# Loading a head group's q and k by twelve sixteen-row DMAs in place of sixteen

## The reference, cut to what matters

```python
x = x + layernorm(attention(layernorm(x)))      # causal, 16 heads, per batch of 1024 tokens
x = x + layernorm(moe(layernorm(x)))            # 8 experts, top 2, 256 -> 1024 -> 256
# attention, per head h:
attn = softmax(mask(q_lat[h] @ c_kv.T / 4)) ;  y[h] = (attn @ c_kv) @ v_eff[h]
```

## Time and profile before

| what | value |
|---|---|
| median of three runs | 1412.35 us |
| the profiled execution, its own time | 1411.45 us |
| its span in the profile | 1409.8 us |
| PE busy | 1124.4 us (80%) |
| DVE busy | 817.6 us (58%) |
| ACT busy | 654.0 us (46%) |
| POOL busy | 586.1 us (42%) |
| DMA moved | 190.07 MB, 135 GB/s on average |

### The profile page before, as it was taken

One profiled execution on the slowest core, in us unless ns is written; L12 is line 12 of the kernel. 1 busy time (PEld: TensorE's weight loads), 2 busy tenths in 40 slices (PEclk: granted clock), 3 DMA queues, 4 the chain that ended last, 5 costly groups with the idle time before them and its releaser, 6 DMA issues. The chain is left out here.

```text
span 1409.8 us, 26281 instructions
## 1 busy us (share of the span) xinstructions
PE 1124.4 (80%) x7809; PEld 834.2 (59%) x7809; DVE 817.6 (58%) x2044; ACT 654.0 (46%) x1111; POOL 586.1 (42%) x675
## 2 busy tenths in 40 slices
PE   5956299998999899999983443099999999999910
PEld 3523255555555555555541433099999999999910
DVE  5626166665666566666622975055555555555567
ACT  2620055554555455555564543044444444444444
POOL 4204055555555355555574577412222222222227
PEclk9977599999999999999997555589999999999965
DMA  4953133343344434443223514342344142341173
GB/s 153 375 217 122 45 136 128 130 141 132 135 143 144 145 127 144 143 144 126 91 91 122 198 67 134 95 157 84 129 168 168 45 168 91 122 168 46 45 253 119
DMA packets 93853, 190.07 MB, mean 135 GB/s; under 512 B 27604, under 2 KB 58596, under 8 KB 85508
## 3 DMA queue, kind: packets, MB, share of 16 engines
q1 hardware_dynamic: 82912, 163.09, 32.7%
q0 software_dynamic: 7680, 22.09, 4.6%
q10 hardware_dynamic: 3176, 3.84, 0.9%
HBM read 109.44 MB, written 79.02 MB: 134 GB/s over the span
## 5 line engine op out<-in xcount | busy, mean ns | idle before, releaser
L775 ACT ACTIVATE att_pt<-att_ps_s 128x1024 f32<-128x1024 f32 (+3 forms) x384 | 305.4, 813 | 250.8 <-PE att_ps_s L690 248.3
L805 DVE TENSOR_REDUCE att_pm<-att_ps_m 128x1 f32<-128x512 f32 (+1 forms) x512 | 298.5, 649 | 125.4 <-PE att_ps_m L657 115.5
L1513 ACT ACTIVATE moe_hf<-moe_ps_h,moe_b 128x256 f32<-128x256 f32 x288 | 136.9, 475 | 222.9 <-PE moe_ps_h L1469 216.2
L653 PE MATMUL att_ps_m<-att_k,att_q 128*128 128x512 f32 (+3 forms) x576 | 202.6, 409 | 39.4 <-DMA att_v<-vs 31.8
L603 POOL TENSOR_SCALAR_AFFINE_SELECT att_pt<-att_pt 128x512 f32<-128x512 f32 x128 | 80.7, 636 | 293.9 <-ACT att_pt L775 293.9
L690 PE MATMUL att_ps_s<-att_q,att_k 128*128 128x512 f32 (+3 forms) x576 | 169.3, 378 | 12.3 <-ACT att_pt L775 6.3
L653 PEld LDWEIGHTS att_ps_m<-att_k,att_q 128*128 128x128 f32 x576 | 114.5, 202 | 81.1 <-DVE att_pm L805 44.1
L1422 POOL DMA_INDIRECT ys<-moe_o,moe_home x72 | 74.0, 1028 | 186.3 <-DVE moe_o L1552 173.3
L690 PEld LDWEIGHTS att_ps_s<-att_q,att_k 128*128 128x128 f32 x576 | 92.0, 191 | 64.0 <-issue 30.8
L1546 DVE TENSOR_TENSOR moe_hTl<-moe_hf,moe_hTh 128x256 fp32r<-128x256 f32 x288 | 123.9, 430 | 10.0 <-DVE moe_hTh L1544 0.2
L657 PE MATMUL att_ps_m<-keep_future,keep_identb 128*128 128x128 bf16 x512 | 118.4, 238 | 0.0
(11 more groups left out here) (196 smaller groups left out, 2587.4 us busy)
## 6 DMA issues: line engine op xcount, KB each, us to landing
att_raw<-in_w SPq DMA_DIRECT2D x16, 1024.0 KB, 5.4
ws<-att_raw_hi SPq DMA_DIRECT2D x16, 1024.0 KB, 5.0
ws<-att_raw SPq DMA_DIRECT2D x16, 1024.0 KB, 6.8
moe_rows<-xs SPq DMA_DIRECT2D x38, 258.0 KB, 2.7
weights_w_0h<-ws SPq DMA_DIRECT2D x8, 1024.0 KB
weights_w_0l<-ws SPq DMA_DIRECT2D x8, 1024.0 KB
att_q<-qs SPq DMA_DIRECT2D x44, 128.0 KB
att_k<-ks SPq DMA_DIRECT2D x44, 128.0 KB
```

The lines of the kernel that those rows point to most:

```text
L653: ins = pe.matmul(out[:, end:end + keys], qg[slot][:, h // 2, i * P:(i + 1) * P], kg[slot][:, h, k0:k0 + keys], start=True, stop=not diag)
L775: act.activation(pt[:, blk % NPT, 2 * p:2 * p + 2, off:CH], ps_s[k % 2][:, :, off:CH], ACT.Exp, scale=HS ** -0.5).then_inc(ex_done, 1)
L805: return dve.tensor_reduce(pm[:, g % 2, place, h:h + 1], src, AX.X, ALU.max)
L1513: act.activation(hf[:, f % NHB], ps_h[f % NHB][:], ACT.Relu, bias=b1[r][:, f:f + 1]).then_inc(hf_done, 1)
```

## The change

For each group the sixteen DMAs of q and k (four for each head) become twelve. Before, each head had: q high (16 rows), q high and low together (32 rows, the source's outermost dimension being the two parts), k high and low together (32 rows), k high (16 rows). After, there are six for each half e of the partitions. Each goes to sixteen partitions and takes the rows of two heads, e and e + 2, of one part (16 x 2 rows of 4 KB, 128 KB). The bytes are the same: 1.5 MB a group. The DMAs that set rows of ones, that of v, the waits and all queues stay as they are.

```diff
-LOADS = 16 * (4 * GH + 3) // NSL
+LOADS = 16 * (2 * 6 + 3) // NSL
...
-    for h in range(GH):
-        head = g % NG * GH + h
-        r, c = 64 * (h % 2), slice(head * HS, (head + 1) * HS)
-
-        for dst, src in ((qg[r:r + HS, h // 2, :], qs[0, c]), (qg[r + HS:r + KR, h // 2, :], qs[:, c]),
-                         (kg[r:r + 2 * HS, h, :], ks[:, c]), (kg[r + 2 * HS:r + KR, h, :], ks[0, c])):
-            sp.dma_start(dst.bitcast(F32), src).then_inc(loaded, 16)
+    heads = slice(g % NG * GH * HS, (g % NG + 1) * GH * HS)
+    q_hi, q_lo, k_hi, k_lo = (t[part, heads].rearrange("(p e c) t -> e c p t", e=2, c=HS) for t in (qs, ks) for part in range(2))
+    for e in range(2):
+        rows = [slice(64 * e + n * HS, 64 * e + (n + 1) * HS) for n in range(3)]
+
+        for dst, src in ((qg[rows[0]], q_hi), (kg[rows[0], e::2], k_hi), (qg[rows[1]], q_hi), (kg[rows[1], e::2], k_lo),
+                         (qg[rows[2]], q_lo), (kg[rows[2], e::2], k_hi)):
+            sp.dma_start(dst.bitcast(F32), src[e]).then_inc(loaded, 16)
```

## The result

The changed kernel takes 1390.76 us (median of four; 1390.33 to 1391.9), the one before on the same chip 1411.86 (four runs). The ratio is 0.9839, 95% interval 0.9827 to 0.9851: 21 us faster. I had forecast 1370.6, range 1365 to 1379: the sign was right, the size double what came, and the time lies 11.8 us beyond the range.

What follows compares the result with a forecast made beforehand. The core was taken to stand still behind group 1's load, on two DMA engines, with ACT's issues in `project` second; 7.0 + 1.5 + 31.8 + 1.5 = 41.8 us off 1411.45, plus 0.9 for the median, gave 1370.6, range 1365 to 1379.

Steps and rivals of the forecast that it cites:

- A: ACT's issue time in `project`: 12 issues of 0.5 us in place of sixteen, gain 7.0 us (5.3 to 9.1).
- B: Group 0's first unit no longer waits 1.51 us for its load; gain 1.5 us (0 to 1.5).
- C: Group 1's first unit: its load lands before PE comes, so the whole 31.8 us wait goes.
- rival 1: Group 1's first unit: sixteen partitions at a time are a bottleneck, 0 to 6.5 us wait stays; 1375; chance 0.2.
- D: PE's clock in group 1's units: without the gap it stays off the lower level; gain 1.5 us (0.5 to 2.5).
- E: Steady groups: loads stay hidden and nothing waits for SP's saved issue time; zero gain.
- 2: Loads of q and k: the new DMAs still run on two engines; about 1445 us, slower than before; chance 0.04.
- 3: `project`: A's gain stays out, an issue costing over 0.64 us or another engine ending the block; 1375.6; chance 0.1.

## Why the prediction was wrong

**A, right.** 7.0 forecast; the block's end moved from 107.28 to 99.80, 7.5, of which 6.8 are ACT's gap. An issue cost 0.45 us, I had taken 0.5; the backlog's 3.6 went.

**B, right.** 1.5 forecast, 1.6 measured: from 109.96 to 100.91 is 9.05, less 7.5.

**C, the step that failed.** "I take 'landed before 132.6', and the 31.8 us go whole." 18.0 of them went, 13.8 stayed. Two things were wrong in it. The rate: I took 180 GB/s from a burst of 0.3 us, and for groups 1 and 2 the sustained rate is 114 to 130. The burst's weak slice, which I had as the lower end, gives the right figure, but that may be chance: sixteen packets from one short DMA say little of a queue of twelve. Nor was 180 out of reach. Group 0's load moves at 162 to 184 GB/s from 78 to 84 us, in six more profiles with the same load there at 123 to 156; group 1's has 182 from 108 to 110 us, then 121. What makes the difference no run tells. The order: even at 114 GB/s my bound was 6.5 us of remaining wait, since I put v at a flat 2.5 us. v stands last and is made of 272-byte packets, and beside group 2's 4 KB packets it took from about 122 us to 138.8. Where group 2's load waits, group 1's has landed by 124, v included. With v first 1.6 us are left, though q and k move no faster (0.69 MB on ACT's queue from 112 to 118 us, 0.73 in the changed kernel). So this rate alone would have cost the forecast little; v's place cost 12.

The Trainium skill's page "SBUF — State Buffer", section "Door 1: The DMA port swizzle", which I had put to rival 1, gives 104 GB/s for sixteen adjacent partitions at 1 MiB. The runs show 114 to 135 for them in `attend`, 165 with every third and 251 with every seventh, with the same bytes and sources: there its direction is borne out, and its figure is somewhat low for this kernel. The load in `project`, up to 184, does not fit it. Weighing it against a burst, I gave it a fifth.

**D, nothing gained.** 1.5 forecast. The idling of the remaining wait brought the clock back to 0.50 until after 150 us, and the first scores moved from 179.38 to 152.55: 26.8, which is A, B and C's 18.0 less 0.3.

**E failed.** "Zero gain" (that is, no change) in steady groups was right for waits of PE on loads, and wrong as a whole: "nothing waits for SP there" left out what SP does next. In the old kernel two DMA engines were late with the load, and so the split weights' stores ended on these two: 8.85 us from the first store's issue to the raw fetch's (465.02 to 473.87), 7.13 after the change (440.01 to 447.14). The raw fetch moved up by 1.7 us against PE and got in front of its instructions: 4.4 us in the two turns. That it is the old loads which lengthen this stretch the kernel with old loads in the loop shows (8.4 us at both turns; 7.1 in the changed kernel); that two late engines are the reason I read from the engines' shares (before, 0.17 and 0.12 from 471 to 473 us; after, 0.12 and 0.03 in the like microseconds), it wasn't tried alone; that the fetch's place makes the turns long is shown.

**The rest.** `attend` ended 23.8 us earlier; 20.6 were left when the experts began, since `route` took 151.3 us in place of 148.0. Two more profiles of the same kernel have 150.1 and 148.8 there, so this scatters from execution to execution, by a wait of PE for instructions among others. Of what the forecast missed (20.7 between the spans' 21.1 and 41.8) C is 13.8, D 1.8, E 3.8 to 4.4; A and B give back 0.6, and the rest of 1 to 2 is within this scatter. By the sign that I had set, more than 3 us of change behind 180 us, the forecast fails as a whole: it was 5.7.

**The rivals.** 1 was the right kind, a slow load with part of the wait left, but it had 0 to 6.5 us for it where 13.8 stayed, and `max_rows` was not late; 2 is out (all engines in use); 3 is out (issues of 0.45 us).

## What to carry to other kernels

Before a DMA is spread over all engines, ask which partitions each of them writes and what rate that gives over the whole transfer; a burst in the trace is no rate. When two queues are in flight together, try the small packets first: here v, 0.28 MB beside 1.57 of q and k, ended last. And when a transfer off the critical path gets faster, look at what its queue issues next and at what that runs into.

## What the runs showed of the hardware

- Sixteen engines writing to sixteen adjacent partitions carry 114 to 135 GB/s in `attend`, whether one or two such loads are in flight; every third partition 165, the same with the two halves in turn 211, every seventh over both halves 234 to 251. The same adjacent load in `project` has 162 to 184 GB/s in one profile and 123 to 156 in six others, for no reason that a run shows.
- Two queues with work do not share the engines by bytes: from 124 to 130 us 226 packets of SP's queue carry 0.65 MB, 297 of ACT's 0.10. Nor do they always take turns: from 112 to 118 us ACT's has 271 packets and SP's 3, with DMAs issued on both.
- At the loop's turn PE waits 2.9 to 3.6 us for instructions, and 4.7 to 6 us when a 1 MB fetch is issued 1.2 to 2.2 us ahead of it.
- TensorE's clock fell to its lower level although PE worked: in the kernel with every seventh partition it was 0.50 from 118 to 126 us with PE busy 8.00 of 8; from 114 to 118 us, at 0.84, PE had been busy 3.52 of 4. The same kernel run again had 1.00 from 114 to 126 us, with PE busy 3.50 of 4 at first. Why is open. It cost little, since DVE set the pace: it is busy 7.79 of the 8 us.

```profile
118.00:122.00 4.00, 4.00 (x13) 2.34 (x12) 3.79 (x7) 0.00 (x0) 0.31 (x1) 0.50 1.01 258
122.00:126.00 4.00, 4.00 (x13) 2.27 (x11) 4.00 (x8) 0.00 (x0) 0.00 (x0) 0.50 0.95 253
```
